# Column tiles for two products of a linear attention, and three layer loops written out

## The reference, cut to what matters

```python
Qp, Kp = _favor_phi(q, omega[l]), _favor_phi(k, omega[l])      # 16 features a head
kv = einsum('bhclm,bhcld->bhcmd', Kc, Vc)                      # sums of keys times values by chunk
kv_pre, ks_pre = cumsum(kv) - kv, cumsum(ksum) - ksum          # over the chunks before
scores = where(mask, einsum('bhcim,bhcjm->bhcij', Qc, Kc), 0)
num = einsum('bhcij,bhcjd->bhcid', scores, Vc) + einsum('bhcim,bhcmd->bhcid', Qc, kv_pre)
den = scores.sum(-1) + einsum('bhcim,bhcm->bhci', Qc, ks_pre)
a = num / (den + 1e-6)
h1 = layer_norm(out + a @ Wo + bo);  out = layer_norm(h1 + relu(h1 @ W1 + bf1) @ W2 + bf2)
```

## Time and profile before

| | us |
|---|---|
| median of 3 runs (lowest, highest) | 3831.24 (3824.48, 3834.24) |
| the profiled execution, its own time | 3831.35 |
| its span, first to last instruction | 3829.6 |
| TensorE busy with matmuls (39640 of them, and as many loads) | 3485.5 (91%) |
| VectorE (DVE) busy | 2636.2 (69%) |
| ScalarE (ACT) busy | 1703.6 (44%) |
| GpSimd (POOL) busy | 901.5 (24%) |
| mean granted TensorE clock | 0.972 |

### The profile page before, as it was taken

How to read it: one execution, slowest core, us unless ns; L and a number is a source line. 1 busy time by engine, 2 the same in 40 slices (tenths; PEclk the granted TensorE clock), 3 DMA queues, 4 the chain that set the end, 5 groups by cost and what they waited for, 6 DMA issues and landing times. The chain is left out here.

```text
span 3829.6 us, 103815 instructions
## 1 busy us (share of the span) xinstructions
PE 3485.5 (91%) x39640; PEld 2723.9 (71%) x39640; DVE 2636.2 (69%) x6838; ACT 1703.6 (44%) x3438; POOL 901.5 (24%) x781
## 2 busy tenths in 40 slices
PE   4999999999999999799958999999999999987998
PEld 3767676767676777688846777777777777756887
DVE  3565655555655555588866778878888788867787
ACT  2555555555555555433323444444434444422332
POOL 3232323232323232100001332232223222320000
PEclk9999999999999999899979999999999999988999
DMA  3000000000000000000000000000000000000000
GB/s 88 29 24 28 24 28 24 28 24 28 24 28 24 28 23 23 12 1 0 1 14 16 2 16 2 2 16 2 16 3 2 16 2 3 2 2 1 1 0 22
DMA packets 38420, 60.41 MB, mean 16 GB/s; under 512 B 6960, under 2 KB 16688, under 8 KB 37552
## 3 DMA queue, kind: packets, MB, share of 16 engines
q1 hardware_dynamic: 37936, 53.78, 4.3%
HBM read 18.10 MB, written 2.10 MB: 5 GB/s over the span
## 5 line engine op out<-in xcount | busy, mean ns | idle before, releaser
L658 ACT ACTIVATE a_prob<-a_s,a_shift,a_scale 128x128 f32<-128x128 f32 (+3 forms) x512 | 311.5, 612 | 483.6 <-DVE a_shift L741 483.4
L1538 ACT ACTIVATE ffn_silu<-ffn_ps_g 128x512 f32<-128x512 f32 x272 | 161.2, 599 | 382.5 <-PE ffn_ps_g L1488 370.2
L1481 PEld LDWEIGHTS ffn_ps_y<-moe_down,ffn_hidden 128*128 128x128 f32 x2176 | 282.1, 191 | 40.0 <-issue 18.5
L1481 PE MATMUL ffn_ps_y<-moe_down,ffn_hidden 128*128 128x128 f32 x2176 | 288.1, 275 | 16.0 <-DVE ffn_acc L1642 16.0
L940 POOL TENSOR_TENSOR t_rstd<-t_var_eps,minus_half 128x4 f32<-128x4 f32 x96 | 97.7, 1017 | 834.9 <-DVE t_var_eps L1252 834.9
L1190 ACT COPY t_num<-t_n 128x512 f32<-128x512 f32 x96 | 56.2, 585 | 515.4 <-PE t_n L1001 514.8
L1642 DVE SCALAR_TENSOR_TENSOR ffn_acc<-ffn_ps_y,ffn_combine,ffn_acc 128x128 f32<-128x128 f32 x960 | 270.5, 347 | 7.7
L1654 DVE TENSOR_TENSOR ffn_hidden<-ffn_silu,ffn_ps_u 128x512 f32<-128x512 f32 x272 | 186.1, 686 | 106.5 <-ACT ffn_silu L1538 74.5
L409 POOL TENSOR_TENSOR a_k_sin<-a_k_swap,sin_swap 128x512 f32<-128x512 f32 x64 | 81.7, 1277 | 721.6 <-DMA a_k_swap<-a_k_own 721.6
L738 DVE TENSOR_REDUCE a_neg_max<-a_s 128x2 f32<-128x256 f32 (+3 forms) x256 | 208.8, 816 | 59.9 <-PE a_s L561 56.7
L1327 DVE TENSOR_TENSOR t_mixed<-t_s,upto 128x512 f32<-128x512 f32 x384 | 238.4, 684 | 14.5 <-PE t_s L977 12.4
(11 more groups left out here) (209 smaller groups left out, 8813.1 us busy)
## 6 DMA issues: line engine op xcount, KB each, us to landing
a_k_swap<-a_k_own SPq DMA_DIRECT2D x128, 128.0 KB, 2.1
a_y_swap<-a_y_own SPq DMA_DIRECT2D x128, 128.0 KB, 2.0
a_staged<-in_pairs SPq DMA_DIRECT2D x8, 384.0 KB, 3.1
t_next<-in_t_w SPq DMA_DIRECT2D x12, 256.0 KB, 3.1
t_next_rows<-in_t_rows SPq DMA_DIRECT2D x6, 448.0 KB, 4.1
x<-in_x SPq DMA_DIRECT2D x8, 256.0 KB, 4.5
out<-x SPq DMA_DIRECT2D x1, 2048.0 KB, 8.7
t_next_sq<-in_t_sq SPq DMA_DIRECT2D x6, 256.0 KB, 2.6
```

The costliest lines, as they stand in the source:

```text
L658: nc.scalar.activation(prob[c % 2][h][:, 0:(c + 1) * P], ps[f"s{h}"][:, 0:(c + 1) * P], ACT.Exp, bias=shift[:, k:k + 1], scale=scale[slot. ...
L1481: t = nc.tensor.matmul(ps_y[e % 2][:, c * P:(c + 1) * P], hidden[e % 3][:, c * P:(c + 1) * P], w_down[:, e * P:(e + 1) * P], start=True, s ...
```

## The change

1. *sums* on TensorE: four column tiles. Strip r of the features (32 columns of `k_tok`) is multiplied by its own two heads' values only (18 columns a span), and goes to partitions 32r to 32r+31. Both halves fit in bank w0. Bank w1 is no longer filled by this step. There are 32 matmuls in the program where there were 8.
2. *sums* on VectorE: the first spans are copied, three additions make the running sums of the 18-column blocks in `k_sum`, reading the bank, and then two multiplications by `own_head`, with the blocks repeated four times, write `kv`. A0 waits for these two.
3. *scores*: one matmul for each head of a strip, 32 rows by 64 columns, to its own half of the partitions. 64 in the program for each of S0 and S1 where there were 32. The results stand where they stood.
4. `pipeline` calls `layer` for every pair or layer in a Python loop: no hardware loop is left in the instruction streams that both attention stages build with it.

```diff
-    with e.Fori(0, plan.LAYERS - 1) as l:
-        layer(l, False)
-    layer(plan.LAYERS - 1, True)
+    for l in range(plan.LAYERS):
+        layer(l, l == plan.LAYERS - 1)
...
-    FILLS = dict(... sums="w0 w1", ...)
+    FILLS = dict(... sums="w0", ...)
...
-    HALF = H // 2 * V
+    PAIR = 2 * V
...
+        k_sum = sb("k_sum", [P, 2, SPANS - 1, PAIR])
...
                         for r in range(4):
-                            mm = nc.tensor.matmul(ps[f"s{r}"][:, u * SPAN:(u + 1) * SPAN],
-                                                  kz[t][strip(r), u, :, :].rearrange("p h n -> p (h n)"),
-                                                  phi_q[parity][t][strip(r), u * SPAN:(u + 1) * SPAN], start=True, stop=True)
+                            for p in range(2):
+                                mm = nc.tensor.matmul(ps[f"s{r}"][p * SPAN:(p + 1) * SPAN, u * SPAN:(u + 1) * SPAN],
+                                                      kz[t][strip(r), u, p, :],
+                                                      phi_q[parity][t][strip(r), u * SPAN:(u + 1) * SPAN],
+                                                      start=True, stop=True)
...
-                        wait(pe, "kv_sum", slot, 3)
+                        wait(pe, "kv", slot, 2)
...
-                        for t_, bank in enumerate(("w0", "w1")):
+                        for bank in ("w0", "w1"):
                             ready(bank, "keys")
-                            free(bank)
+                        free("w0")
+                        for t_ in range(2):
                             for c in range(TILES):
                                 n = 2 if c < TILES - 1 else 1
-                                t = nc.tensor.matmul(
-                                    ps[bank][:, 2 * c * HALF:(2 * c + n) * HALF].rearrange("p (s n) -> p s n", s=n),
-                                    k_tok[:, t_, c, :],
-                                    v_tok[:, c, 0:n, 8 * t_:8 * t_ + 8, :].rearrange("p s h d -> p s (h d)"),
-                                    start=True, stop=True)
-                            t.then_inc(filled[bank], 1)
+                                at = (t_ * (SPANS - 1) + 2 * c) * PAIR
+                                for r in range(4):
+                                    t = nc.tensor.matmul(
+                                        ps["w0"][strip(r), at:at + n * PAIR].rearrange("p (s n) -> p s n", s=n),
+                                        k_tok[:, t_, c, strip(r)],
+                                        v_tok[:, c, 0:n, 8 * t_ + 2 * r:8 * t_ + 2 * r + 2, :]
+                                        .rearrange("p s h d -> p s (h d)"), start=True, stop=True)
+                        t.then_inc(filled["w0"], 1)
...
+                        full("w0")
+                        new = ps["w0"][:, 0:2 * (SPANS - 1) * PAIR].rearrange("p (t s n) -> p t s n", t=2, n=PAIR)
+                        nc.vector.tensor_copy(k_sum[:, :, 0:2, :], new[:, :, 0:2, :]).then_inc(s["k_sums"], 1)
+                        for c in range(1, TILES):
+                            wait(dve, "k_sums", slot, c)
+                            at = slice(2 * c, min(2 * c + 2, SPANS - 1))
+                            n = at.stop - at.start
+                            t = nc.vector.tensor_tensor(k_sum[:, :, at, :], new[:, :, at, :],
+                                                        k_sum[:, :, 2 * c - 1:2 * c, :].broadcast_to([P, 2, n, PAIR]),
+                                                        ALU.add)
+                            t.then_inc(s["k_sums"] if c < TILES - 1 else emptied["w0"], 1)
+                        wait_emptied(dve, "w0", slot, "sums")
+                        for t_ in range(2):
                             nc.vector.tensor_tensor(
-                                kv[:, :, 8 * t_:8 * t_ + 8, 0:V],
...
+                                kv[:, :, 8 * t_:8 * t_ + 8, 0:V].rearrange("p u (r h) n -> p u r h n", r=4),
+                                k_sum[:, t_, :, :].rearrange("p u (h n) -> p u h n", h=2).unsqueeze(2)
+                                .broadcast_to([P, SPANS - 1, 4, 2, V]),
...
+                                .broadcast_to([P, SPANS - 1, 4, 2, V]), ALU.mult).then_inc(s["kv"], 1)
```

More of the change, by code:

```diff
@@ L768 @@
     WITH = dict(Wo_norm="Wo", F2_norm="F2")
-    FILLS = dict(weights="", turn="w0", project="w1 w0", values="n1", mapq="s0 s1", mapk="s2 s3", keys="w0 w1", sums="w0 w1",
+    FILLS = dict(weights="", turn="w0", project="w1 w0", values="n1", mapq="s0 s1", mapk="s2 s3", keys="w0 w1", sums="w0",
                  S0="s0 s1 s2 s3", S1="s0 s1 s2 s3", A0="n0", A1="n1",
@@ L854, in transformer_block @@
         emptied = {k: sem("emptied_" + k) for k in plan.BANKS}
-        EVENTS = dict(o_now=1, o_bias=1, kz=4, kv_sum=3, v_tok=1, v_pad=1, den=2, inv=2,
+        EVENTS = dict(o_now=1, o_bias=1, kz=4, k_sums=3, kv=2, v_tok=1, v_pad=1, den=2, inv=2,
                       stats=8, mv=8, eps=2, rstd=2, xn=8, scaled=2, h1b=1, o_new=1)
-        PHASE = {n: "in" if n in ("o_now", "kz", "kv_sum", "v_tok", "v_pad") else "mix" if n in ("den", "inv") else "out"
+        PHASE = {n: "in" if n in ("o_now", "kz", "k_sums", "kv", "v_tok", "v_pad") else "mix" if n in ("den", "inv") else "out"
                  for n in EVENTS}
@@ L1291, in body @@
                     elif step == "sums":
-                        for t_, bank in enumerate(("w0", "w1")):
-                            full(bank)
-                            nc.vector.tensor_tensor(
-                                kv[:, :, 8 * t_:8 * t_ + 8, 0:V],
[L1296 to L1308, removed]
-                                                    .broadcast_to([P, n, H, V]), ALU.add).then_inc(s["kv_sum"], 1)
+                        full("w0")
@@ new lines, in body @@
+                        wait_emptied(dve, "w0", slot, "sums")
+                        for t_ in range(2):
+                            nc.vector.tensor_tensor(
+                                kv[:, :, 8 * t_:8 * t_ + 8, 0:V].rearrange("p u (r h) n -> p u r h n", r=4),
+                                k_sum[:, t_, :, :].rearrange("p u (h n) -> p u h n", h=2).unsqueeze(2)
+                                .broadcast_to([P, SPANS - 1, 4, 2, V]),
+                                mem["own_head"][:].rearrange("p (r h n) -> p r h n", r=4, h=2).unsqueeze(1)
+                                .broadcast_to([P, SPANS - 1, 4, 2, V]), ALU.mult).then_inc(s["kv"], 1)
@@ L1373, in _ @@
                 dve.sem_inc(made_out["dve"], 1)
-                begin(dve, "kv_sum stats mv eps xn den inv kz v_tok v_pad")
+                begin(dve, "k_sums kv stats mv eps xn den inv kz v_tok v_pad")
                 pipeline(dve, plan, weights_in, weights_out, body, plan.DVE)
```

## The result

The changed kernel takes 3884.35 us (median of 4 runs, 3880.61 to 3885.47), the kernel before 3829.22 (4 runs, 3824.48 to 3834.24): ratio 1.0137, 95% interval 1.0125 to 1.015. It is slower by 55 us (1.4%) where 52 less were forecast. The profiled execution took 3884.17 us, its span is 3882.4.

A forecast was written before the change was run, and what follows sets the result against it. TensorE was taken to set the slot, standing still at loop jumps and for the instruction supply (122 matmuls in about 3.05 us). Terms -26.4 + 6 - 19.6 - 12 = -52 from 3831.35 gave 3779 us, range 3700 to 3832.

The forecast's parts named there:

- Loops, stage a: Writing out stage a's loop removes six jumps back of 4.4 us, -26.4 us; some 48 slots becoming straight cost +6.
- Rival D: Writing out the loops brings nothing, as straight code waits for its packets instead: 3819 us, chance 0.07.
- Loops, stage b: Writing out stage b's loop removes four jumps back of 4.9 us, -19.6 us; straightness itself gives 0.1 us a slot.
- sums: In stage b's slot, S0 begins about 1.05 us after sums on TensorE; VectorE's sums take 2.4 us instead of 3.0.
- S0 and S1, "16 x 65 = 1.04 us": The split scores' 128 matmuls run in 16 rounds of eight tiles at 65 ns, 1.04 us where 1.94 stood.
- Rival B: Small matmuls go no faster than 16 ns, so S0 and S1 keep 2.0 us: 3808 us, chance 0.20.
- Stops: TensorE waits for instruction packets: some 1.75 us in 0.42 of S0, 1.3 in 0.15; A0 to turn takes 4.65 us.
- Clock, "a fall in one slot of ten": In stage b the clock falls after stops in one slot of ten, up to 1.7 us each: 0.15 us a slot.
- rival C: Stops in S0 and S1 lower the clock in most slots, up to 1.7 us each: 3850 us, chance 0.08.
- C's sign: What would show the falling clock: the clock at 0.50 in most slots, stage b's mean below 0.8.
- The signs named at the end: Signs of being right, among them some 390 instruction packets and S1 in two pieces with stops of 1 to 2 us.
- Rival A: Instructions are no bound and packets come in time, so a slot takes 26.2 us: 3657 us, chance 0.13.

The follow-up runs named there:

- e1: The kernel before with the loops of both attention stages written out and nothing else: 3800.26 us, ratio 0.9909.
- e2: The changed kernel with the scores put back in their old tiles (loops out and new sums stay): 3770.57 us, ratio 0.9831.
- e10: The same as e9 without any added wait, so the packet edge creeps from slot to slot: 3779.48 us, ratio 0.9868.
- e5: e1 with 34 always-fulfilled waits in each full slot of stage b, holding a packet edge just before S1: 3883.41 us, ratio 1.014.
- e6: e5 with 113 more always-fulfilled waits, once before stage b's first slot, moving the packet edge into turn: 3792.61 us, ratio 0.9902.
- e9: The changed kernel with old score tiles, sums in two column tiles of 64, and added waits placing the packet edges: 3744.8 us, ratio 0.9771.
- e7: e2 with S1 moved ahead of nums in TensorE's order: 3817.89 us, ratio 0.9962.

## Why the prediction was wrong

**Loops, stage a (-26.4 and +6).** Right: -20.4 forecast, -19.2 measured, the slots 23.4 us apart (23.8 at the end of a pair), no "issue" of 3 us between them and no clock at 0.50. Rival D is out.

**Loops, stage b (-19.6, and 0.1 us a slot for straightness).** Wrong in its parts: e1 shows -12.6 where about -24 were forecast. The 4.9 us were taken from two slots at a layer's end against two inside, and put down to the jump whole. But most of the difference belongs to the layer's end: of the 2.9 to 3.4 us of the jump 1.40 us remain as a wait for ScalarE, and behind it the clock is at its low level in both (20.5 us in all before, 17.1 in e1). The two slots about each jump are 1.0 us shorter together in e1, not 4.9; it is the slots inside the layers that gain, about 0.3 us each, where the forecast gave them 0.1. Why those gain was not traced.

**sums.** Right on both engines: TensorE 1.11 us to S0 (forecast 1.05). The timeline of VectorE, the slot of the second stop above, answers to the earlier trace rows:

```profile
2789.15 0.23 DVE L1299 COPY t_k_sum<-t_w 128x72 f32<-128x72 f32 x1
2789.42 0.73 DVE L1304 TENSOR_TENSOR t_k_sum<-t_w,t_k_sum 128x72 f32<-128x72 f32 x3
2790.19 1.28 DVE L1310 TENSOR_TENSOR t_kv<-t_k_sum,own_head 128x504 f32<-128x504 f32 x2
2791.38 1.19 DVE L1324 COPY t_v_pad<-t_v_tok 64x256 f32<-64x256 f32 x4
2792.60 2.48 DVE L1333 TENSOR_TENSOR t_mixed<-t_s,upto 128x512 f32<-128x512 f32 x4
```

2.23 us from the copy to `v_pad` (forecast 2.4), and the masks end at 2795.08, 6.74 after sums begins (forecast 7.15). e2 was forecast right too.

**S0 and S1, "16 x 65 = 1.04 us".** This term failed. Without a stop and at full clock the 128 matmuls take 1.37 to 1.38 us from the first start to the last, 87 ns a round of eight, and 1.51 us to the start of F2, the measure by which the 1.94 of before was taken; that is between my value and the other bound of 2.0. The rows of the same shape along the columns had rounds of two tiles; eight are not as fast as two. 0.47 us in S1, and in the 0.57 of the S0 where the sum let TensorE and not VectorE hold A0: about 35 us in 48 slots. Rival B (16 ns a matmul) is out as well: 10.8 ns.

**Stops.** The sum came out near by luck of its parts. Forecast: 0.42 x 1.75 + 0.15 x 1.3 = 0.93 us in S0 and 4.65 - 1.89 - 1.04 = 1.72 from A0 to turn, 48 x 2.65 = 127 us (115 after what S0's stops share with the wait for VectorE). Measured: 53.4 + 63.2 = 117 in the scores, 146 with the edges in other steps. The rule behind it was wrong: I asked for a whole packet begun and ended inside the burst, and the time from edge to edge. Every S0 is a packet long and holds an edge, and stops come in 39 of 48, not in 27, also where the edge lies 26 to 61 matmuls into S0, while the packet that ends there reaches back through sums into F1 and keys and took 3.6 to 9.7 us: by my rule there could be none. The records of the instruction queue show more: ahead of a stop the transfer is seen to begin only 2.2 to 2.8 us before TensorE resumes, as a rule well inside the packet before, not at its start. The last 192 instructions ahead of a stop took, with the stop itself, 1.9 to 3.8 us, mostly about 2.8; the split scores pass as many in 1.0 us. As a rule that isn't enough either: edges in the first 19 matmuls of S1 mostly pass without a stop though their last 192 took 1.4 to 1.8 us, and so do nearly thirty edges of e10. Ahead of edges in A0 in e10 the transfer had begun before the last edge, a packet earlier. What decides when a transfer begins stays open. That the place of the edge decides the time, e5 and e6 show, and e9 and e10.

**Clock, "a fall in one slot of ten": 0.15 us a slot.** This step failed too. The text took the mean clock of stage b as a sign that stops mostly aren't followed by a fall; with 78 stops of 1.5 us in place of 32 of 0.6 they were. The 107 us more at the 1.2 GHz level can cost up to half of that, 54 us, an estimate. In the table F2 is 0.67 us a slot longer than in e2 and turn to project 0.33, together 48 us, of which 14 are stops at edges in these steps: 34 us of clock that can be seen, against the 7 forecast. It is rival C's mechanism near its size: 160 us are 47 lengths of 3.4 us in 48 slots, 31 more than before, or 0.65 a slot, where C counted on 0.75 to turn the sign. Here the pace, the stops and the loops of stage b helped to turn it. C's sign, a mean clock of stage b below 0.8, could not have shown it: one fall of 3.4 us in a slot of 30 leaves 0.94, and 0.95 was measured.

Added up for stage b, where 32 us less were forecast and 66 more were measured, a gap of 97: loops 12, pace 35, clock 27, stops 146 - 115 = 31. That is 105, an estimate whose parts overlap where a stop falls into a low clock. Stage a adds 1 us and the rest of the program 6.

**The signs named at the end.** 365 packets came instead of some 390: what the scores and sums ask for is there (352 x 48 / 256 = 66, and 365 against the 299 of e1 is 66), but written-out loops need 27 fewer (299 against 326), which I had not taken off. S1 in two pieces in nearly every slot, with stops of 1 to 2 us, was right (39 of 48, 1.6 us on average).

Rival A is out: the supply of instructions does hold the kernel up. The Trainium skill (Runtime: NRT & Kernel Launch, Instruction fetch mechanics) has the next block of 256 instructions fetched while the present one is executed, and says that this is hidden, as issue is slower. The size of the blocks agrees with the stops at every 256th instruction; that it is hidden does not, where a matmul and its load pass in 11 ns.

## What to carry to other kernels

Tiles that run side by side save array time and multiply instructions: before splitting a matmul, count the loads and matmuls that it adds to a burst. Here a step of 256 of them, which passed in 1.4 us by itself, held a stop at 39 of 48 packet edges, of 0.5 to 2.7 us, with a fall of the clock behind many; a step of 128 (e2, 1.74 us by itself) behind a fast A0 held one at 20 of 24. What was worth more is a slot whose instructions are a multiple of 256 with the edge laid into slow work: e9 takes 3744.8 us, 2.3% less than the kernel before and 3.6% less than the change. When a step is moved away from such a burst, ask first which wait it was covering (e7). The same holds for a loop's jump: what it covers comes to light when it goes (e1).

## What the runs showed of the hardware

- The place of a packet edge is a cost of its own: the same loads and matmuls took 3883.41 or 3792.61 us, depending on 113 idle instructions issued once (e5, e6). So a change of a few instructions anywhere ahead can shift a kernel of this kind by a per cent or two without touching its work.
- Eight tiles of 32 rows by 64 columns take 87 ns a round of 64 moving columns (128 matmuls start within 1.37 us), four tiles of 32 by 128 take 111 (64 within 1.74 us); with their loads the small ones pass at 10.8 ns a pair.
- Waits that are always fulfilled aren't free everywhere: the four ahead of F1's first matmul, where TensorE has just been waiting, cost 0.4 us a slot (from keys to F1 1.22 us in e1, 1.64 in e6), while the 12 among F1's others and the 18 among F2's cost nothing that shows (F1 to sums 3.54 and 3.51 us, F2 3.67 either way).
